# Context and projections in f32, keys split by GpSimd, and search pieces of 128 query rows in four 32-column blocks

## The reference

```
layer 0 attention (32 score heads of 4 numbers, 16 value heads of 8):
  q = LN(x) @ Wq.T;  k = ctx @ Wk.T;  v = ctx @ Wv.T
  a1 = softmax(q1 k1 / 2) v;  a2 = softmax(q2 k2 / 2) v     # 16 heads each
  out = RMSnorm_per_head(a1 - lambda * a2) * subln * (1 - 0.238..) @ Wp.T + bp
layer 1 attention (16 heads of 8, biases, a mask over the keys):
  out = softmax(mask(q k / sqrt(8))) v @ Wo.T + bo
feed-forward: router over 8 experts, top 2, silu experts (layer 0 with a shared one)
```

## Time and profile before

| | |
|---|---|
| median of 3 runs | 2584.38 us (2583.19 to 3398.32) |
| the profiled execution | 2582.84 us, of which the profile's span is 2581.0 us |
| mean granted TensorE clock in the span | 0.953 of full speed |
| layer 0 attention, from about 100 us to 1371 us | TensorE 97% busy between 400 and 1200 us |
| layer 1 attention, from about 1547 us to 2420 us | TensorE 97% busy between 1700 and 2200 us |

### The profile page before, as it was taken

One profiled execution on the slowest core, in us unless ns is written; L12 is line 12 of the kernel. 1 busy time (PEld: TensorE's weight loads), 2 busy tenths in 40 slices (PEclk: granted clock), 3 DMA queues, 4 the chain that ended last, 5 costly groups with the idle time before them and its releaser, 6 DMA issues. The chain is left out here.

```text
span 2581.0 us, 66889 instructions
## 1 busy us (share of the span) xinstructions
PE 2352.3 (91%) x28024; PEld 1277.8 (50%) x28024; DVE 1802.4 (70%) x3165; ACT 1466.8 (57%) x2101; POOL 770.1 (30%) x926
## 2 busy tenths in 40 slices
PE   3699999999999999999995976999999999999798
PEld 2244444444444444444444852555555555555576
DVE  2588888887887888888864554767667767676454
ACT  2156666666666666666673322665566666656422
POOL 4213323333333243233323442121212122221232
PEclk8589999999999999999997986999999999999799
DMA  3533434534534434444401106565566565653100
GB/s 93 109 66 78 96 95 80 101 90 77 110 77 90 105 77 95 98 80 99 97 2 48 32 29 124 109 117 112 114 116 120 110 123 115 127 107 65 50 1 14
DMA packets 152931, 222.40 MB, mean 86 GB/s; under 512 B 45156, under 2 KB 102116, under 8 KB 152132
## 3 DMA queue, kind: packets, MB, share of 16 engines
q1 hardware_dynamic: 152644, 218.29, 40.5%
HBM read 141.39 MB, written 76.48 MB: 84 GB/s over the span
## 5 line engine op out<-in xcount | busy, mean ns | idle before, releaser
L959 ACT ACTIVATE probs<-score_ps 125x896 f32<-125x896 f32 x1152 | 1012.5, 917 | 261.0 <-PE score_ps L863 260.3
L1021 DVE TENSOR_REDUCE max_part<-max_ps 112x1 f32<-112x500 f32 x1538 | 992.2, 670 | 238.9 <-PE max_ps L844 129.3
L879 PE MATMUL acc_ps<-probs,vext 125*32 125x224 f32 (+1 forms) x12288 | 676.4, 315 | 7.1 <-issue 6.2
L1021 DVE TENSOR_REDUCE max_part<-spare_ps 112x1 f32<-112x500 f32 x766 | 513.5, 670 | 118.0 <-PE max_ps L844 105.5
L844 PE MATMUL max_ps<-kstack,qstack 48*112 48x500 f16 x1538 | 518.1, 401 | 25.7 <-DVE max_part L1021 12.9
L879 PEld LDWEIGHTS acc_ps<-probs,vext 125*32 125x32 f32 x12288 | 257.7, 108 | 305.9 <-issue 281.1
L863 PE MATMUL score_ps<-qstack,kstack 50*125 50x224 f16 (+1 forms) x6144 | 386.9, 243 | 1.9 <-ACT probs L959 1.7
L863 PEld LDWEIGHTS score_ps<-qstack,kstack 50*125 50x125 f16 x6144 | 303.6, 134 | 111.4 <-issue 53.4
L844 PE MATMUL spare_ps<-kstack,qstack 48*112 48x500 f16 x766 | 307.0, 401 | 14.9 <-DVE max_part L1021 7.2
L844 PEld LDWEIGHTS max_ps<-kstack,qstack 48*112 48x112 f16 x1538 | 167.0, 128 | 197.6 <-DVE max_part L1021 132.3
L740 POOL TENSOR_TENSOR heads_out<-turned,rden 56x64 f32<-56x64 f32 x192 | 55.2, 288 | 695.6 <-DVE rden L1012 685.5
(11 more groups left out here) (185 smaller groups left out, 2537.3 us busy)
## 6 DMA issues: line engine op xcount, KB each, us to landing
kstack<-k_parts SPq DMA_DIRECT2D x384, 187.5 KB, 6.5
k_parts<-khl SPq DMA_DIRECT2D x128, 375.0 KB, 5.5
ctx_in<-in_ctx SPq DMA_DIRECT2D x32, 750.0 KB
context_parts<-ctxT SPq DMA_DIRECT2D x32, 750.0 KB, 4.8
ctxT<-context_parts SPq DMA_DIRECT2D x32, 750.0 KB, 6.1
qrows<-q_parts SPq DMA_DIRECT2D x384, 7.0 KB, 7.4
qstack<-max_rows SPq DMA_DIRECT2D x384, 0.9 KB
mask_in<-in_mask SPq DMA_DIRECT2D x64, 82.0 KB
```

Source lines behind the costliest of these rows:

```text
L879: last = nc.tensor.matmul(acc_ps[32 * j:32 * j + 32, TT * S * i:TT * S * (i + 1)].rearrange("p (s c) -> p s c", s=S), vext[n % SLOTS][:, t ...
L959: nc.scalar.activation(probs[t % 2][:, 896 * h:896 * h + 896].rearrange("k (b c) -> k b c", b=2), score_ps[(t * H + h) % 2][0:KT, :, 0:448 ...
L1021: nc.vector.reduce_max(max_part[0:PIECE, u, third:third + 1], room(user)[0:PIECE, 0:TK], AX.X).then_inc(s_red, 1)
```

## The change

- Context: T's copy is f32 (one ScalarE copy, no low part), stored to DRAM as f32 (the same number of bytes). Layer 1 has two context buffers and issues a context load one sequence earlier. V and K take the f32 context and f32 weights: one matmul in place of three. The f16 weight parts of the set-up are gone.
- Layer 1's K is copied by ScalarE to f32 with the bias, and GpSimd splits it, as in layer 0.
- Layer 0's pieces are 128 query rows: 14 tiles x 3 = 42 pieces for a sequence. As 128 rows cross the 224-column groups, a piece is four matmuls of 32 query rows, each on a 64-row x 32-column part of the array; the blocks of the two pieces of a pair are issued in turn, after both rooms have been waited for. 21 pairs lie in 24 places; the second pair is left out in steps 2, 6 and 10. Layer 1's pieces stay 112 rows and one matmul.
- `where` is new: side 1 has one user in every step of layer 0 (F was on side 0).
- `fill_m` issues 4 DMAs in place of 8 in layer 0.

```diff
-        self.parts = self.group_cols // PIECE
-        self.tiles = 2 * PAIRS * self.parts
+        self.piece = 112 if masked else 128
+        self.tiles = self.cols // self.piece
...
-        ctx_in = sb("ctx_in", [KT, NKT, D])
-        ctxT = sb("ctxT", [128, 2, SK], F16)
-        w_parts = sb("w_parts", [128, 2, 2, 2, D], F16)
+        ctx_f = sb("ctx_f", [128, 2, NKT * D])
+        wk_order = sb("wk_order", [128, D])
...
-        where = {("V", 0): (0, 1), ("F", 0): (1, 0), ("V", 1): (1, 1), ("F", 1): (2, 0), ("V", 2): (2, 1),
-                 ("T", 0): (3, 1), ("K", 0): (4, 1), ("T", 1): (5, 1), ("K", 1): (6, 1), ("M", 0): (7, 0), ("T", 2): (7, 1),
-                 ("K", 2): (8, 1), ("A", 0): (9, 1)}
+        where = {("V", 0): (0, 1), ("F", 0): (1, 1), ("F", 1): (2, 1), ("V", 1): (3, 1), ("T", 0): (4, 1), ("V", 2): (5, 1),
+                 ("K", 0): (6, 1), ("M", 0): (7, 0), ("T", 1): (7, 1), ("K", 1): (8, 1), ("T", 2): (9, 1), ("K", 2): (10, 1),
+                 ("A", 0): (11, 1)}
...
-        where = {("V", 0): (0, 1), ("F", 0): (1, 0), ("V", 1): (1, 1), ("F", 1): (2, 0), ("V", 2): (2, 1),
-                 ("M", 0): (7, 0), ("K", 0): (7, 1), ("K", 1): (8, 1), ("K", 2): (9, 1), ("A", 0): (10, 1)}
+        where = {("V", 0): (0, 1), ("F", 0): (1, 1), ("V", 1): (2, 1), ("F", 1): (3, 1), ("V", 2): (4, 1), ("K", 0): (5, 1),
+                 ("K", 1): (6, 1), ("M", 0): (7, 0), ("K", 2): (8, 1), ("A", 0): (10, 1)}
...
+    slots = -(-L.pieces // (2 * NKT))
+    unused = NKT * slots - L.pieces // 2
+    spread = NKT * slots // unused if unused else NKT * slots + 1
...
+        d, slot = (1, (AHEAD + t) * slots + k) if t < NKT - AHEAD else (2, (t - NKT + AHEAD) * slots + k)
+        if k >= slots or slot % spread == spread - 1 or n + d >= B:
             return []
...
-                    for k, (w, x) in enumerate(((0, 0), (1, 0), (0, 1))):
-                        last = nc.tensor.matmul(spare_ps[:, 0:TK], Wk[w], ctxT[:, x, TK * i:TK * i + TK], start=k == 0, stop=k == 2)
+                    nc.tensor.matmul(spare_ps[:, 0:TK], Wk[:, :], ctxT[n % len(ctxT)][:, TK * i:TK * i + TK],
+                                     start=True, stop=True).then_inc(s_ready, 1)
...
-                        for k, (x, w) in enumerate(((0, 0), (0, 1), (1, 0))):
-                            last = nc.tensor.matmul(spare_ps[0:KT, D * t:D * t + D], ctxT[:, x, c:c + KT], Wv[w],
-                                                    start=k == 0, stop=k == 2)
+                        last = nc.tensor.matmul(spare_ps[0:KT, D * t:D * t + D], ctxT[n % len(ctxT)][:, c:c + KT], Wv[:, :],
+                                                start=True, stop=True)
...
+                    wait_for_room(("P", n, p))
+                    r, third, k, _ = piece(p)
...
-                    if not L.masked:
-                        wait_for_room(("P", n, p))
-                    nc.tensor.matmul(room(("P", n, p))[0:PIECE, 0:TK], qstack[n % SLOTS][rows, c, PIECE * i:PIECE * (i + 1)],
-                                     kstack[n % SLOTS][rows, c, TK * third:TK * third + TK],
-                                     start=not L.masked, stop=True, skip_group_check=True).then_inc(s_piece, 1)
+                width = 32 if L is L0 else L.piece
+                for j in range(L.piece // width):
+                    for _, n, p in pair:
+                        r, third, k, _ = piece(p)
+                        rows = slice(HALF * r, HALF * r + KROWS)
+                        c, start = divmod(k * L.piece + j * width, GC)
+                        last = nc.tensor.matmul(room(("P", n, p))[width * j:width * (j + 1), 0:TK],
+                                                qstack[n % SLOTS][rows, c, start:start + width],
+                                                kstack[n % SLOTS][rows, c, TK * third:TK * third + TK],
+                                                start=not L.masked, stop=True, skip_group_check=True)
+                        if j == L.piece // width - 1:
+                            last.then_inc(s_piece, 1)
...
-                    nc.scalar.activation(ctxT[:, 0, TK * i:TK * i + TK], spare_ps[:, 0:TK], ACT.Copy).then_inc(s_ctxT, 1)
+                    nc.scalar.activation(ctxT[0][:, TK * i:TK * i + TK], spare_ps[:, 0:TK], ACT.Copy).then_inc(s_ctxT, 1)
...
-                if kind == "T":
-                    k = slice(TK * i, TK * i + TK)
-                    dve.wait_ge(s_ctxT, NTHIRD * n + i + 1)
-                    nc.vector.tensor_tensor(ctxT[:, 1, k], spare_ps[:, 0:TK], ctxT[:, 0, k], ALU.subtract).then_inc(s_cl, 1)
```

More of the change, by code:

```diff
@@ L201, in _ @@
                     link(nc.vector.tensor_scalar(small[f"bp{i}"][:, :], small[f"bp{i}"][:, :], tg[:, i:i + 1], None, ALU.mult))
[L202 to L211, removed]
+                    link(nc.vector.tensor_scalar(small[f"WkT{i}"][:, :], small[f"WkT{i}"][:, :], QK_UP, None, ALU.mult))
+                link(nc.vector.tensor_copy(wk_order[:, :].rearrange("p (r h x) -> p r h x", r=2, h=2), halves_first(small["WkT0"][:, :])))
                 link(nc.vector.tensor_scalar(small["bk1"][:, :], small["bk1"][:, :], QK_UP, None, ALU.mult))
@@ L231, in build @@
         for L in (L0, L1):
-            for kind in ("context", "mask"):
-                T[f"{L.name}_{kind}_loaded"] = sem(f"{L.name}_{kind}_loaded")
+            T[f"{L.name}_mask_loaded"] = sem(f"{L.name}_mask_loaded")
+            T[f"{L.name}_context_loaded"] = [sem(f"{L.name}_context_loaded{i}") for i in range(1 + L.masked)]
         normalise(T, "norm0", 0)
@@ L478, in attend @@
     qstack = [T["qstack"][i][:, 0:PAIRS * GC].rearrange("p (c q) -> p c q", c=PAIRS) for i in range(SLOTS)]
-    Wk, Wv = ([T["w_parts"][:, layer, w, part, :] for part in range(2)] for w in range(2))
+    Wk, Wv = (small["WkT1"] if L.masked else T["wk_order"]), small[f"WvT{layer}"]
     S = L.heads // VH
@@ L637, in fill_m @@
                 sp.wait_ge(s_mr, n + 1)
+                half = L.tiles // 2
                 for part in range(2):
@@ L640, in fill_m @@
                         row = HALF * r + KROWS + part
-                        for i in range(L.parts):
-                            u = (i * 2 + r) * PAIRS
-                            sp.dma_start(qstack[n % SLOTS][row:row + 1, :, PIECE * i:PIECE * (i + 1)],
-                                         max_rows[u:u + PAIRS, part, 0:PIECE]).then_inc(s_mrow[n % SLOTS], 16)
+                        sp.dma_start(qstack[n % SLOTS][row:row + 1, :, :].rearrange("a c q -> a (c q)"),
+                                     max_rows[half * r:half * (r + 1), part, 0:L.piece]).then_inc(s_mrow[n % SLOTS], 16)
             def next_context(n):
@@ L761, in _ @@
             for n in range(3):
[L762 to L763 removed]
+                split_keys(n)
                 if n < 2:
@@ L770, in _ @@
                     finish(n)
-                if L is L0 and n + 3 < B:
+                if n + 3 < B:
                     split_keys(n + 3)
@@ L984, in drain @@
                 kind, n, i = user
-                if kind in "VAF" or (kind == "K" and L is L0):
+                if kind != "M":
                     return
@@ L1016, in reduce_piece @@
                 _, n, p = user
-                r, third, c, i, u = piece(p)
+                r, third, _, u = piece(p)
                 if p == 0:
@@ L1101, in feed_forward @@
     hidden = [carve(k2, NTT * D + CW * i, [CW]) for i in range(HS)]
-    gate = [T["ctxT"][:, i, 0:2 * CW].bitcast(F32) for i in range(2)]
+    gate = [T["ctx_f"][:, i, 0:CW] for i in range(2)]
     tmp = [T["probs"][0][0:TT, CH * D * i:CH * D * i + CH * D].rearrange("p (t d) -> p t d", t=CH) for i in range(DB)]
```

108 lines of the change are left out of this document (41 added, 67 removed).

## The result

The changed kernel takes 2628.03 us (median of 4, 2625.85 to 2628.72) where the kernel before takes 2585.3 beside it: ratio 1.0167, 95% interval 1.0147 to 1.0187. It is 1.7% slower. (One of the kernel before's four runs, 3398 us, was in the slower state of the chip and is left out of the ratio.) The forecast was 2574: the time lies inside the range and inside the 2% that stood as most likely, but 54 us above the forecast and on the other side of no change.

A forecast was written before the change was run, and what follows sets the result against it. Layer 0 was taken as bound by TensorE's written order with waits for rooms VectorE frees, layer 1 as nearly TensorE alone. Layer 0, layer 1 and start: 2582.8 - 36 + 25 + 1 = 2573, stated as 2574 us; range 2505 to 2645.

The forecast's parts named there:

- full drain: Layer 0: if each of 12 added shape changes drained TensorE, 0.19 us each, 1.5 us a sequence worse.
- A room is free for TensorE some 0.06 after the reduction's end: Both layers' searches: TensorE can use a room about 0.06 us after VectorE's reduction on it ends.
- 0.06 on scores to search: Layer 0, each step: 0.06 us added between scores and search pair for changing the array's shape.
- 0.02 for issue: Layer 0, each search pair: 0.02 us extra for issuing eight block matmuls that run side by side.
- K and V: f32 projections on TensorE: K to the scores 0.96 us for 0.74, V to the scores 1.03 for 0.84.
- second, a pair now waits for both rooms: Layer 0: a search pair starts only when both rooms are free, making first pair to second 1.19 us.
- the sum of its waits: Layer 1, waits behind VectorE's low part of K: some 0.2 us in each of steps 8 to 10, 0.3 in step 11.
- Rival 1: Layer 0's blocks or shape changes cost more: slower, 2658 us with full drain and more issue, 2980 with blocks in turn; chance 0.17.
- Rival 2: VectorE is the true bound of layer 0: faster, 2526 us with half its savings, 2445 with all; chance 0.2.
- Rival 3: Layer 1's f32 projections hide behind waits, so the +25 us is nothing: 2549 us; no separate chance given.
- Rival 4: Small blocks make the chip grant 1.2 GHz in layer 0: over 3000 us; chance 0.03.
- a few stalls: Layer 1 before the change: 25.5 us a sequence in the profile with stalls, 25.1 by the count of steps.

The follow-up runs named there:

- the swap: The changed kernel with the two waits of a layer-0 pair written in the other order, second piece's room first: 2595.46 us, ratio 1.0047 to the kernel before.
- experiment 5: The kernel before with only layer 0's new search (common wait kept) and new order of users; f16 projections, layer 1 as it was: 2593.04 us, ratio 1.0014.
- experiment 3: The changed kernel, but each layer-0 piece waits only for its own room, its blocks issued piece by piece: 2566.24 us, ratio 0.9911 to the kernel before.
- experiment 8: As experiment 7, but without the split of layer 1's K by GpSimd: 2526.23 us, ratio 0.9751 to the kernel before.
- experiment 6: The kernel before with only layer 1's K copied by ScalarE to f32 and split by GpSimd: 2580.64 us, ratio 0.9977.
- experiment 7: The kernel before with layer 0's 128-row pieces, own-room waits and new user order, plus layer 1's GpSimd split; f16 projections: 2527.14 us, ratio 0.9769.
- experiment 9: As experiment 7, but layer 1's F users moved from steps 1 and 2 to steps 3 and 4: 2507.05 us, ratio 0.9686 to the kernel before.

## Why the prediction was wrong, step by step

*Right.* The eight blocks of a pair run side by side. The order of TensorE's groups bounds layer 0, with room waits in it, and VectorE idles more (69% busy). Layer 1 becomes slower by the f32 passes, the clock stays, GpSimd's splits are hidden and the search waits for no keys. The size of a change of shape was of the right kind, a little, though 0.09 to 0.10 us and not 0.06. The Trainium skill, TensorEngine Tiling, "Key Properties", says that changing the tiling mode drains the engine. The measured 0.09 to 0.10 is half of the prediction's estimate for a full drain, 0.19, so it neither bears the page out nor excludes a partial drain.

*Wrong, layer 0: 39.61 against 38.1, 1.5 us a sequence.* Three terms:
- "A room is free for TensorE some 0.06 after the reduction's end". That holds where a room's wait stands by itself. With two waits ahead of one pair, the wait for the reduction became an instruction of its own, and TensorE starts 0.14 to 0.15 after the reduction. It decides ten times a sequence: 0.91 us, shown by the swap. This is the largest term, 33 of the 54 us, but it doesn't turn the sign alone: with the order of the waits put right the kernel measures 1.0047, still slower by 12 us where the forecast was faster by 10.
- "0.06 on scores to search" and "0.02 for issue", 12 x 0.06 + 21 x 0.02 = 1.14 us a sequence, or 1.20 with 24 pairs. Measured with 24 pairs is 1.53, of which 0.09 to 0.10 a step lies at scores to search: +0.3.
- K and V. K to the scores was taken as 0.96 and V as 1.03; they are 1.03 and 1.07, +0.3 in all. TensorE in layer 1 of the changed kernel, a V and a K with the scores after them:
```profile
1808.68 1.14 PE L793 MATMUL max_ps<-wide,ctx_f 128*125 128x128 f32 x8
1809.75 0.40 PE L845 MATMUL score_ps<-kstack 56*125 56x448 f16 x2
...
1818.35 1.10 PE L788 MATMUL max_ps<-ctx_f,wide 128*128 128x500 f32 x2
1819.38 0.40 PE L845 MATMUL score_ps<-kstack 56*125 56x448 f16 x2
```
The three make 1.57 for the 1.51 that is to be told. Some of K's and V's goes into waits that were there: their spacings add 3 x 0.29 + 3 x 0.23 = 1.6 over f16, and 0.82 arrives (experiment 5). So that the three add up this closely is in part luck.

*Priced, but never weighed:* "second, a pair now waits for both rooms". Its 1.19 came out (1.20 in the swap). What the forecast didn't ask is what layer 0 would be without it: 0.7 us a sequence and some at the start, 29 us. The prediction took the common wait as part of the pieces' price, and so missed the larger thing: with the waits of experiment 3 and f16 projections layer 0 comes to 37.25 (experiment 8), 2.1 us a sequence under before.

*Layer 1: 26.34 against 25.9.* K and V again, 3 x 0.07 + 3 x 0.04 = 0.33 of 0.44. The other 0.1 is the forecast's own addition: its listed terms sum to 26.0, not 25.9 (and those of layer 0 to 38.0, not 37.9). The gain from the split was priced well: the sum of its waits, some 0.9 us, against 0.78 in experiment 6.

*The rivals.* Rival 1, slower, had the direction. It put the cost at the blocks, which are 0.3 us a sequence above the price, not at the release, which is 0.9. Rival 2 fell with experiment 3: with its waits gone from TensorE, the kernel gains 62 us while VectorE stays at 70%. Rival 3 fell: layer 1 pays. Rival 4 fell: the clock is 1.00 in both stretches.

*Seen, but not priced:* the stops. The prediction speaks of "a few stalls" in layer 1 and sums undisturbed steps. That does no harm to its sum, as the changed kernel has about as many as the kernel before (long steps of 10.7 and 10.2 us). But the split's gain was real in the undisturbed steps and lost in the stops. The trace ties them to the loading of the program: each ends 1.2 to 1.9 us after a packet of an instruction queue, and in the one shown the packet came 14 us after the packet before it, while the DMA engines were full. A denser sequence uses its instructions up sooner, which fits experiments 6, 7 and 9. It isn't density alone that brings them: experiment 5 has 6 stops in a layer 1 with the old program, where the kernel before has 3.

*Open:* no run changed the loading alone, so why a packet comes late, and why spreading the users helps, is argued from the traces and not shown. Nor was it parted what the blocks cost beyond scores to pair.

## What to carry to other kernels

Ask of every wait that is put ahead of a group which of its parts could start without it, and let each piece wait only for its own room; where two waits must stand together, the late one belongs on the instruction that does the work, which here is the wait that the kernel names first. Judge f32 against three f16 passes by the spacing from its start to the next group, in which its first weights are included, and only where TensorE has slack. When a steady step is made shorter and the time stays, look for stops that the median step doesn't show.

## What the runs showed of the hardware

- Of two waits ahead of one weight load, one is an instruction by itself. If that is the late one, the pair starts 0.145 us after the reduction, else 0.055: ten times a sequence, 33 us here.
- Eight f16 matmuls of 48 x 32 weights and 500 columns start within 0.03 us and let the next group in 0.34 behind the first, as two of 48 x 112 do (0.33). The price of blocks is 0.13 us a step, 0.09 to 0.10 of it between the scores and the first of them.
- With DMA engines full, TensorE stopped for 1.8 us for nothing that the profile's waits show, and was granted 0.55 of its clock for 4.5 us after. It went on 1.38 us after a packet of an instruction queue had ended; the 45 such stops in eleven kernels all ended 1.2 to 1.9 us after one.
